# Making each scatter of routed records wait for the landing of the one before it

## What is computed

```
attention, per batch and head (16 heads of 8 features):
  xc = x - mean over tokens;  corr = softmax(xc xc^T);  out = corr x
experts, over all 4096 tokens:
  scores = sigmoid(x gate^T);  sfc = scores + bias
  keep 4 of 8 groups (by the sum of a group's two best sfc), in them the 8 best of 64 experts
  weight of a chosen expert = 2.5 * score / sum of the 8 scores
  an expert takes its first 128 assignments, in token order; later ones are dropped
  out = sum over a token's experts of weight * w2(silu(w1 x) * (w3 x)) + shared expert(x)
```

## Time and profile before

| | |
|---|---|
| median of 3 runs | 831.56 us (830.72 to 834.9) |
| profiled execution | 831.34 us, span from first to last instruction 829.6 us |
| busy | PE 446.8 us, ACT 385.9, POOL 382.1, DVE 336.7 |
| L504, the record scatters | 256 issues, 251.2 us busy on POOL, first at 97.5, last at 653.6 |
| L527, the accumulating scatters | 64 issues, 99.0 us busy on POOL, first at 677.5, last at 794.2 |
| idle of ACT before L906 | 223.1 us, 163.9 of it until a release that the trace cannot name ("remote") |

### The profile page before, as it was taken

How to read it: one execution, slowest core, us unless ns; L and a number is a source line. 1 busy time by engine, 2 the same in 40 slices (tenths; PEclk the granted TensorE clock), 3 DMA queues, 4 the chain that set the end, 5 groups by cost and what they waited for, 6 DMA issues and landing times.

```text
span 829.6 us, 8798 instructions
## 1 busy us (share of the span) xinstructions
PE 446.8 (54%) x2932; PEld 198.1 (24%) x2932; DVE 336.7 (41%) x1102; ACT 385.9 (47%) x516; POOL 382.1 (46%) x431
## 2 busy tenths in 40 slices
PE   4888842972396179527831983396115275564100
PEld 4232300330132023102300320032114264453100
DVE  5336721661365038304720660264462253333236
ACT  2989821972395159317921873294001152221016
POOL 2000275047306710770175037406747428888846
PEclk9999955995598569757975896597557586767555
DMA  3999810000000000000000000000000245544378
GB/s 99 228 295 188 163 51 7 1 19 9 4 1 21 3 1 13 6 4 1 16 3 1 1 15 3 1 4 13 2 14 2 77 122 76 92 55 37 35 182 240
DMA packets 83123, 43.64 MB, mean 53 GB/s; under 512 B 13319, under 2 KB 82707, under 8 KB 83072
## 3 DMA queue, kind: packets, MB, share of 16 engines
q1 hardware_dynamic: 61568, 36.18, 18.3%
q0 software_dynamic: 21504, 6.81, 7.2%
HBM read 21.27 MB, written 44.40 MB: 79 GB/s over the span
## 4 chain that ended last, share of the span: by engine, by line
PE 23%; another core or an unknown queue 22%; ACT 19%; issue 13%; POOL 12%; DVE 9%; DMA 1%; SPq 0%; ACTq 0%; POOLq 0%; DVEq 0%
ACT large L906 14%; POOL sums L527 12%; PE S L658 7%; PE PV L672 6%; PE M L578 3%; ACT OT L891 2%; PE M L776 2%; PE PV L682 1%; PE M L607 1%; ACT LR L884 1%; DVE large L1396 1%; PE M L601 1%; DVE last_stats L1480 1%; PE M L620 1%
## 5 line engine op out<-in xcount | busy, mean ns | idle before, releaser
L906 ACT ACTIVATE large<-S,shift_now 128x1024 f32<-128x1024 f32 x256 | 276.5, 1122 | 223.1 <-remote 163.9
L504 POOL DMA_INDIRECT records<-rec,index x256 | 251.2, 981 | 212.1 <-DVE index L1296 136.5
L658 PE MATMUL S<-LR 64*128 64x512 bf16 x512 | 110.0, 431 | 172.7 <-ACT large L906 119.4
L672 PE MATMUL PV<-large,V 128*9 128x512 f32 x1024 | 153.3, 674 | 0.2 <-ACT large L906 0.2
L527 POOL DMA_INDIRECT sums<-centred,target x64 | 99.0, 1547 | 42.1 <-DVE centred L1449 22.9
L658 PEld LDWEIGHTS S<-LR 64*128 64x128 bf16 x512 | 24.7, 94 | 332.9 <-ACT large L906 221.7
L1063 DVE RECIPROCAL rden<-PV 128x16 f32<-128x16 f32 x32 | 8.1, 253 | 204.3 <-remote 186.6
L487 POOL PARTITION_ALL_REDUCE largest_all<-largest x8 | 3.0, 373 | 125.8 <-DVE largest L1125 86.3
L1156 DVE COPY LR<-M 128x1024 bf16<-128x1024 bf16 x42 | 28.8, 686 | 39.3 <-PE M L578 22.9
L682 PE MATMUL PV<-ident,OT 128*128 128x128 f32 x128 | 23.8, 314 | 24.7 <-ACT OT L891 15.6
L803 PE MATMUL PV<-ident,AK 128*128 128x128 f32 x32 | 8.7, 364 | 43.3 <-DVE AK L1422 43.3
(11 more groups left out here) (180 smaller groups left out, 707.6 us busy)
## 6 DMA issues: line engine op xcount, KB each, us to landing
records<-blank SPq DMA_DIRECT2D x1, 6176.0 KB, 29.7
X<-records SPq DMA_DIRECT2D x16, 386.0 KB, 3.4
large<-sums SPq DMA_DIRECT2D x24, 256.0 KB, 4.9
sums<-blank SPq DMA_DIRECT2D x2, 2112.0 KB
large<-L_ffn_w_dram SPq DMA_DIRECT2D x2, 2048.0 KB, 21.6
records<-rec,index POOLq DMA_INDIRECT x256
X<-L_attn_x_dram SPq DMA_DIRECT2D x8, 256.0 KB, 2.9
sums<-Z SPq DMA_DIRECT2D x8, 256.0 KB
```

Source lines behind the costliest of these rows:

```text
L504: pool.indirect_dma_start(records, bass.IndirectOffsetOnAxis(ap=index[:, i * TOP + k:i * TOP + k + 1], axis=0), rec[:, i, :], None, bounds ...
L658: mm = pe.matmul(S[:, 2 * (n % 2) + j, :], LR[rows, pair, 0, tile * P:(tile + 1) * P], LR[rows, pair, 1, :], start=True, stop=True)
L672: mm = pe.matmul(PV[g % 2][32 * i:32 * i + VCOLS, :], V[:, 2 * c + k, QUAD * g + i, :], E[:, u % 2, i, k, :], start=c == 0 and k == 0, sto ...
L906: nc.scalar.activation(E[:, u % 2, 2 * (i // 2):2 * (i // 2) + 2, i % 2, :], S[:, 2 * (n % 2):2 * (n % 2) + 2, :], ACT.Exp, bias=shift_now ...
```

## The change

Ahead of each of the 32 indirect DMAs of `scatter(p)`, POOL waits until `scattered[p % 2]` has reached the count of all scatters issued before it to that semaphore. A DMA adds 16 when it has landed, and `scatters_before(p)` is 16 x 32 for each earlier batch of the same parity.

```diff
@@ -501,6 +501,7 @@
                 wait(pool, post, post_at(p, "index"))
                 for i in range(TILES):
                     for k in range(TOP):
+                        wait(pool, scattered[p % 2], scatters_before(p) + 16 * (i * TOP + k))
                         pool.indirect_dma_start(
                             records, bass.IndirectOffsetOnAxis(ap=index[:, i * TOP + k:i * TOP + k + 1], axis=0),
                             rec[:, i, :], None, bounds_check=last_slot, oob_is_err=False).then_inc(scattered[p % 2], 16)
```

## The result

The changed kernel takes 971.4 us (median of 4, 967.5 to 973.4) against 831.3 us for the kernel before on the same chip: ratio 1.167, interval 1.162 to 1.172.

What follows compares the result with a forecast made beforehand. It took each batch as alternating scatters (41 us, attention nearly still) and attention, routing, index (37 us). With POOL then the bound: first scatter at 97.5, scatters 727.2, gaps 46, fuller rows 10, tail 171.7, say 1053 us; range 945 to 1245.

Steps and rivals of the forecast that it cites:

- Slower, since each scatter pays its landing and POOL becomes the bound: The forecast itself: POOL's record scatters wait for each landing and set the pace, 1053 us against 831.34; chance 0.77.
- Term 1: Record scatters on POOL: period T from 1.28 to 2.9 us, so a batch's scatters take 90.9 instead of 40.6 us.
- Term 2: POOL's work between two batches' scatters: 8.6 us with a reduction, 1.7 us without, 46 us for the seven gaps.
- Term 3: DVE's index for the next scatters: ready in time, a batch's some 48 us of work hidden beneath 91 us of scatters.
- Term 4: From the last scatter's end to the execution's end: 176.7 us less 5 us for earlier weight copying, 171.7 us remain.
- DVE holds the scatters up: Rival at POOL's scatter issues: they cannot proceed beside DVE copies, up to 11 us a batch, 1141 us; chance 0.03.
- The stall as a fixed property of the kernel: Attention idle during dense record scatters, taken as going with them; rival that it stays whatever their spacing: 1244 us, chance 0.14.

Runs made afterwards that it cites:

- a third: Kernel before with at most two scatters in flight and the maximum over partitions taken by PE and DVE instead of POOL: 814.2 us, ratio 0.976.

## Why the prediction was right, and where its sizes were off

- **Slower, since each scatter pays its landing and POOL becomes the bound:** right. POOL waited 364.5 us for landings, DVE up to 50 us for POOL's maximum, and the first scatter stayed at 97.5.
- **Term 1, T = 2.9 us:** too long; measured 2.485 us. The landing of 2.07 us was right (median 2.1). The failing step is the 0.74 us from release to start, taken from a row in which DVE's work ended POOL's wait; behind a landing it was 0.27 us, and the usual period 2.35 us, at the lower bound of 2.37 us that the prediction kept. The 0.1 us for a longer issue was not needed either (median 0.97), and the 1.20 us behind it were put down to an idle POOL, while issues after 26 us of idle time and no reduction took 1.07. The long landings, 29 us in all, made up for a part of this. With the 10 us for fuller rows, which T as measured already holds, the term is off by 248 x (2.485 - 2.9) - 10 = -113 us.
- **Term 2, gaps of 8.6 us:** too short; 14.6 us each. The 6 us ahead of the reduction never show in the trace of before, as there POOL was idle ahead of it anyway: a cost that lay under an idle stretch. 5 x 6.0 = +30 us; the two gaps without a reduction were 1.6 and 1.0 us, 0.8 us less than summed.
- **Term 3, the stall lifts and the index is ready:** right; no "remote" wait is left, and POOL waited for the index once, for the first batch. The reason given, that at 1.85 us a scatter there is none, was never tried on record scatters in a session with the stall.
- **Term 4, the tail, 171.7 us:** 967.5 - 797.0 = 170.5 us, right.
- Together 1052.4 - 113 + 30 - 0.8 - 1.2 = 967.4, against 967.53 us for the profiled execution. The errors of terms 1 and 2 had opposite signs, so the 8% flatter the working.
- **DVE holds the scatters up:** not at the 88 us of the rival, but not never, as the prediction's "I add nothing" had it. With nearly all of DVE's work beside them the issues took a median of 974 ns, before 972, and a mean of 992, before 981; the lengthened ones (8 here, 21 in the kernel before without the stall, up to 1.65 us) all lie beside DVE work. The four issues of the earlier trace rows were too few to see it. Whether the rule that the prediction cited from the Trainium skill (SBUF — State Buffer, SBUF: two separate sides) is the cause no run here tested: as given there it is about two-port copies, and the DVE work beside the longest issues was of several kinds. A part of the long landings may belong here too; periods with 1 us or more of DVE work beside them averaged 2.61 us, those with none 2.39, and one of 3.76 us had none.
- **The stall as a fixed property of the kernel:** wrong, and the prediction's one large blind spot. Its sentence "it stood still in all eight stretches" held for this trace, but half of the sessions have no stall. The forecast survived since the changed kernel has no stall in either kind of session; that the first session was one with the stall, in which 831 us was the number to compare with, was luck. A forecast of the ratio would have missed 1.43.

## What to carry to other kernels

A wait for the landing of one's own last DMA costs landing plus some 0.3 us per issue, less the issue period of today, and this counts in full once the issuing engine is the bound; waiting at every eighth keeps most of the pace (1.44 us against 1.31). When an in-order engine gets busier, look for its costs that lie under its idle time now: here 13 us around the reduction in each batch, which only a busy POOL made visible and only a run without that instruction explained. A mean period hides pauses, so look at the single ones before you name a threshold. And an idle time whose releaser the trace can't name should be looked for on a second chip, in another session, before it is made a term.

## What the runs showed of the hardware that was not expected

- The same program took 678 to 680 us on chips 1 and 7 and 828 to 833 us on chips 2 and 6 (and on the first chip). In the slower sessions ACT and DVE stand idle beside dense indirect scatters for up to 18.6 and 31.8 us at a time, with their inputs ready. In five of the first six batches DVE's long wait ends 4.3 to 4.5 us after the last scatter's issue; ACT comes back for single instructions in between, as at 188.91 and 200.90 us in the batch of the earlier trace rows. The number of packets does not differ, and the issue period hardly: 1.29 us with the stall, 1.31 without.
- In those sessions the stall was there in both kernels with a mean period of 1.29 us and in the batches of a third with means of 1.30 to 1.36 us, weaker in that kernel's batches with 1.47 and 1.50 us, and absent beside the accumulating scatters of L527 at 1.85 us (another kind of DMA, beside other work) and at 2.3 us and above. What POOL's scatters do to the other engines' waits, and what makes one session differ from another, stays open.
- A scatter starts 0.78 to 0.82 us after the end of the DVE instruction that it waits for (1.0 us the first of all), after 1.55 to 33 us of idle time alike, and 0.27 us after a landing.
- The reduction over partitions on POOL, shown as 0.38 us, costs 12.9 us more than a copy in its place by the gaps (14.6 against 1.7 us), and (971.0 - 908.0) / 5 = 12.6 us by the times.
